# Expert stage: a fifth PSUM bank for the up products, one bank for both kinds of transpose, down products five units behind

## The reference, cut to what matters

```python
h = jax.nn.silu(jnp.einsum('ech,ehf->ecf', buf, w1))      # 8 experts, 128 -> 512
out_buf = jnp.einsum('ecf,efh->ech', h, w2)               # 512 -> 128
pair_out = out_buf[flat_e, slot] * keep[:, None]
combined = jnp.sum(pair_out.reshape(N, K, H) * k_probs[..., None], axis=1)
...
x = x + s * silu(combined + xn)
```

## Time and profile before

| | |
|---|---|
| median of 3 runs | 1129.29 us (1127.92 to 1129.47) |
| profiled execution, its own time | 1126.79 us |
| its span, first to last instruction | 1125.0 us |
| TensorE busy in the span | 993.5 us (88%) |
| VectorE, ScalarE, GpSimd busy | 832.7, 775.5, 644.6 us |
| mean granted TensorE clock, full is 1 | 0.968 |
| expert phase's blocks | 935 us to 1092 us from the span's start |

### The profile page before, as it was taken

How to read it: one execution, slowest core, us unless ns; L and a number is a source line. 1 busy time by engine, 2 the same in 40 slices (tenths; PEclk the granted TensorE clock), 3 DMA queues, 4 the chain that set the end, 5 groups by cost and what they waited for, 6 DMA issues and landing times. The chain is left out here.

```text
span 1125.0 us, 18399 instructions
## 1 busy us (share of the span) xinstructions
PE 993.5 (88%) x5064; PEld 426.3 (38%) x5064; DVE 832.7 (74%) x1591; ACT 775.5 (69%) x1524; POOL 644.6 (57%) x781
## 2 busy tenths in 40 slices
PE   4699999998999999869999999999999977888860
PEld 3123333333333332213344444444444354544430
DVE  4588888897888888748777767777777664565555
ACT  1067777776777777647788888888888666676651
POOL 6444545362636333336669787787878640655565
PEclk9999999999999999979999999999999998999995
DMA  2553836041314131369977886877887327112136
GB/s 58 97 89 102 186 98 131 21 81 42 59 28 71 43 48 46 105 184 272 228 206 200 236 231 182 237 208 198 227 226 205 87 89 246 54 57 78 28 99 241
DMA packets 102378, 149.78 MB, mean 133 GB/s; under 512 B 18216, under 2 KB 72088, under 8 KB 101838
## 3 DMA queue, kind: packets, MB, share of 16 engines
q1 hardware_dynamic: 95470, 139.65, 47.2%
q0 software_dynamic: 6272, 8.94, 2.8%
q10 hardware_dynamic: 544, 0.13, 0.2%
HBM read 109.44 MB, written 40.04 MB: 133 GB/s over the span
## 5 line engine op out<-in xcount | busy, mean ns | idle before, releaser
L811 ACT ACTIVATE a_probs<-a_score 128x512 f32<-128x512 f32 x512 | 291.9, 598 | 119.0 <-PE a_score L892 112.0
L987 DVE TENSOR_REDUCE a_mx<-a_mxps 128x2 f32<-128x1024 f32 x256 | 306.6, 1211 | 51.3 <-PE a_mxps L883 46.5
L1585 POOL TENSOR_TENSOR m_hidl<-m_hid,m_hidh 128x512 f16<-128x512 f32 x203 | 234.4, 1168 | 74.4 <-ACT m_hidh L1648 67.0
L1654 ACT ACTIVATE m_h<-m_h 128x512 f32<-128x512 f32 (+1 forms) x264 | 153.7, 583 | 48.7 <-PE m_h L1772 42.6
L1868 DVE TENSOR_TENSOR m_hid<-m_h,p_gates 128x512 f32<-128x512 f32 x196 | 134.0, 688 | 65.2 <-ACT m_h L1654 58.7
L904 PE MATMUL a_ops<-a_probs,a_vst 128*32 128x512 f32 x1024 | 138.1, 612 | 0.0
L1648 ACT ACTIVATE m_hidh<-m_hid 128x512 f16<-128x512 f32 x203 | 126.2, 622 | 11.0 <-DVE m_hid L1868 10.5
L1750 PE MATMUL m_y<-m_hidh,p_wdh 128*128 128x512 f16 (+1 forms) x264 | 100.3, 380 | 9.9 <-POOL m_hidl L1585 7.8
L2154 POOL DMA_INDIRECT t_picked<-e_yrow,p_rows x66 | 65.8, 998 | 75.2 <-DVE e_yrow L2289 55.6
L892 PE MATMUL a_score<-a_qstack,a_kstack 128*128 128x512 f16 x256 | 97.6, 387 | 6.7 <-ACT a_probs L811 3.5
L2302 DVE SCALAR_TENSOR_TENSOR e_hidl<-e_h,e_hidh 128x468 f16<-128x468 f32 (+1 forms) x96 | 57.5, 603 | 60.6 <-ACT e_hidh L2170 47.6
(11 more groups left out here) (308 smaller groups left out, 1933.1 us busy)
## 6 DMA issues: line engine op xcount, KB each, us to landing
p_gates<-t_cw SPq DMA_DIRECT2D x256, 256.0 KB
t_slots<-p_blank SPq DMA_DIRECT2D x8, 723.9 KB
t_qparts<-a_qparts SPq DMA_DIRECT2D x32, 128.0 KB
t_picked<-p_blank SPq DMA_DIRECT2D x8, 512.0 KB
p_raw<-up SPq DMA_DIRECT2D x8, 512.0 KB, 4.9
p_raw<-down SPq DMA_DIRECT2D x8, 512.0 KB, 5.1
p_rows<-t_slots SPq DMA_DIRECT2D x5, 723.9 KB
a_xin<-x SPq DMA_DIRECT2D x8, 256.0 KB, 5.0
```

The source lines that it names most:

```text
L811: act.activation(probs[:, kt % 2, g, :], score[:, g % 2, :], ACT.Exp, scale=SCALE / (QS * QS)).then_inc(exp_done, 1)
L987: dve.tensor_reduce(mx[ahead % 2][:, j // 2, g:g + 2], mxps[:, j % 2, :, :], AX.X, ALU.max).then_inc(mx_done, 1)
L1585: pool.tensor_tensor(hidl[0:r0, k % r, :], hid[0:r0, k % r, :], hidh[0:r0, k % r, :], ALU.subtract).then_inc(lo_done[0], 1)
L1654: act.activation(h, h, ACT.Silu, scale=1.0 / WS).then_inc(silu_done, 1)
```

## The change

`h` gets a fifth bank (`XBANKS` 5), which is taken from the transposes: both kinds now write one bank, `turned`. `down` runs 5 units behind `up` instead of 4. As the transposes share a bank, each kind waits until the other kind's last content has been read: `rows_turned(B)` for `row_done` of block B - 4, `result_turned(B)` for `xl_done` of block B + 3. In the orders, `result_out(B-2)` now comes at f = 0 instead of `result_out(B-1)` at f = 3; `result_turned(B-2)` and `result_rows(B-2)` move from f = 1 to f = 2; `split_weights` moves from f = 2 to f = 1. The final sum over pieces uses five banks as well.

```diff
-XLAG = 4
-XBANKS = 4
+XLAG = 5
+XBANKS = 5
...
-        xps, ops = ps("x", [P, 512]), ps("o", [P, 512])
+        turned = ps("x", [P, 512])
+        xps, ops = turned, turned
...
-                if f == 3 and B:
-                    result_out(B - 1)
+                if f == 0 and B >= 2:
+                    result_out(B - 2)
             high_part(FC * ALL - 1)
+            result_out(ALL - 2)
             result_out(ALL - 1)
...
+                if B >= 4:
+                    pe.wait_ge(row_done, B - 3)
                 for t in range(nt):
                     op = pe.transpose(xps[:, CR * t:CR * t + CR], rows_in[e % XBUFS][:, t0 + t, 0:D], ident[0:CR, 0:CR])
...
                 pe.wait_ge(yc_done, B + 1)
+                pe.wait_ge(xl_done, min(B + 4, ALL))
...
-                if f == 1 and B >= 2:
+                if f == 2 and B >= 2:
                     result_turned(B - 2)
-            result_turned(ALL - 2)
             for g in range(FC * ALL - XLAG, FC * ALL):
                 down(g)
+                if g == FC * ALL - XLAG + 2:
+                    result_turned(ALL - 2)
...
-                if f == 2 and B in SPLIT_IN:
+                if f == 1 and B in SPLIT_IN:
                     split_weights(dve, pre, JOBS + 1 + SPLIT_IN[B])
-                if f == 1 and B >= 2:
+                if f == 2 and B >= 2:
                     result_rows(B - 2)
```

## The result

The changed kernel takes 1153.07 us, the median of four executions, against 1129.11 us of the kernel before in the same session. One of the four took 1514.9 us at a mean granted clock of 0.659, and without it the median is 1150.55 us and the ratio to the kernel before 1.0203, 95% interval 1.0175 to 1.023. The two intervals don't overlap: the kernel before was some 4 us faster in the later session, so the size of the loss is known as 2.0 to 2.6% and no better. It is slower, as forecast; the forecast was 1166 us, with 1147 us for the case that no increment of TensorE is late any more.

The account below looks back on a forecast made before the run. TensorE was taken as the bound. Terms summed to +55.1 us with increments as late and +17.6 with none late; the middle, +36.4 on 1126.8, made 1163.2, and the median standing 2.5 higher gave 1166 us, range 1144 to 1187.

Parts of the forecast that it names:

- nothing late: End of the range where no TensorE increment is late any more: +17.6 us in sum, 1147 us.
- The deciding wait: At block start, TensorE's `rows_turned(B+1)` waits for DVE's `result_rows(B-3)` on the shared bank: 20 stops, 39.1 us.
- The split of the weights: `split_weights` at f = 1 delays DVE's low part in blocks 4, 7 and 10: +2.8 us, between 0 and 5.7.
- The late increments: TensorE's increments reach ACT late at eight places: +7.1 us if they stay as late, -17.2 if they vanish.
- The clock: TensorE's clock falls after long pauses: +5.6 us if increments stay late, -4.2 if none is late.
- my row: Profile row: 13 matmuls against 22 in the next 3.4 us stretch, so a clock fall costs 1.4 us.
- The other new wait: `result_turned` waiting for `x_low`: costed at nothing, with a thin cover of 0.6 us.
- The end: Time until block 20's rows are written: -2.9 us with nothing late, +0.5 with block 22's late place kept.
- A slow clock at every stop: Rival: stops of 1.6 to 2.2 us suffice to slow the clock, +59.7, 1189 us; chance 0.13.
- The covered stop: Rival: `result_rows` is done before TensorE arrives, so the ring's 9 us is had, 1120 us; chance 0.04.
- The third rival: Stops replace the pauses, increments never late: even at 1129 us if a stop costs under 1.1 us; chance 0.03.

Follow-up runs that it names:

- the later session: The unchanged changed kernel measured again beside other runs of the kernel before, giving its second trace: 1.026 (1.0245 to 1.0275), 1153.94 us.
- the variant with four banks: Changed kernel, its order and shared transpose bank kept, with XBANKS and XLAG 4 instead of 5: 1.0269 of the kernel before, 1153.65 us.
- the one with separate banks: Changed kernel's order and lag of five, but two separate transpose banks without the two new waits and four up-product banks: 0.9974, 1120.88 us.
- four variants with a pause at the start of nearly every block: Changed kernel with four banks, 1.0269; with split_weights behind result_rows, 1.021; with DVE's old order, 0.9927; kernel before with a wait in blocks 3 to 22, 1.0017.
- the variant with the rows first: Changed kernel with DVE's result_rows moved ahead of the low part of unit 4B+1: 0.9972 of the kernel before, 1121.37 us.
- the variant with three forced pauses: Kernel before with an added TensorE wait for the low part of unit 4B-2 at blocks 6, 12 and 18 only: 1.0006, 1125.49 us.

## Why the prediction was right, and where its size came from

The direction and the mechanism were right, the size was half as large again as measured: +36.4 us forecast, +23.8 between the profiled executions. The range held it, near its end for nothing late.

**The deciding wait: right, to a few hundredths.** The stops were forecast at 1.73, 2.20 and 1.93 us of lost pace, or 1.57, 2.04 and 1.77 as the trace counts idle time (0.16 less, the pipelined end). The trace has 1.57, 2.02 and 1.75, twenty of them, and that no other part of the change causes them is shown by the variant with four banks and by the one with separate banks. The pace lost is 39.6 us of idle time and 0.15 or 0.16 us for each restart (a matmul's record is 0.36 long while at full pace the next starts 0.20 after it), 42.8 us. The term was 39.1 for the plain stops and 2.8 for the split, 41.9.

**The split of the weights: a little under.** It lengthened three stops from 1.75 to 3.08, 4.0 us instead of 2.8. The second trace has 2.65, which makes 2.7 us, so the term is within what two traces differ by.

**The late increments: the term that made 1166 of 1147.** I had +7.1 if they stayed and -17.2 if they vanished, and took the middle for want of a row. They vanished. That is the term that was mis-sized: it went in at the middle, -5, and measured -17.2 (-19.5 with the restarts, below). The range held because it spanned both ends, not because the prediction knew which end would come. The row was there in part, as I had noted that lateness began at least 6 us after a pause, while the changed kernel runs some 5.4 us at a stretch; the bound was not turned into a weight. The runs show what was behind it: the increments were late only with all of POOL's indirect transfers and a TensorE that had no pause in each block. The changed kernel and four variants with a pause at the start of nearly every block, of 0.3 to 3.1 us, had no late place from block 3 on. Where TensorE's increments wait, and for what, is not shown by any of these runs.

**The clock: wrong.** I said that pauses up to 2.17 us leave the clock alone, and that none of the falls would be left if nothing was late: -4.2. The changed kernel has five falls where the kernel before has three after a pause: three after the stops that the split lengthens, but two after plain stops of 2.02 us, while most stops of the same length have none. In its second trace all five follow plain stops of 2.0. So the length of a single pause doesn't decide. Other traces say the same: a pause of 1.91 us in the variant with the rows first was followed by a fall, one of 2.77 us in the variant with three forced pauses was not. A fall cost 1.68 us, not 1.4. The Trainium skill, "TensorE: Matmul & The Clock Gate", Part 1 and its glossary, gives the penalty as throttled time times (1 - K/N), where K of N clock pulses are let through, 4 of 8 at the lower level: 1.7 us for 3.4. Here the changed kernel's trace agrees with the page, and my row, which compared matmul counts of neighbouring stretches, was too low. Four of the falls lie before unit 88, one more than before: +1.7 us.

**The other new wait.** Costed at nothing, and it was met once, in block 2, for 1.2 us. After that never.

**The end.** -2.9 forecast for nothing late, -1.4 measured to block 20's rows, and the rest of the span 0.9 longer. The fifth fall of the clock lies in this stretch, just behind the start of unit 88; at 1.68 us it is about the whole miss, so the term itself was right.

**The sum again, to unit 88.** 42.8 of stops, -17.2 of old pauses, +1.2, +1.7 of the clock make 28.5; the landmarks give 26.6. The 2 us between them are the restarts of the old pauses: the new stops were counted with 0.16 us for each restart, the old ones without. Between the landmarks there are twelve old pauses, the eleven of the 17.2 us and one of 0.39, so with their restarts 17.2 + 0.4 + 1.9 = 19.5 us went away, and the sum is 26.4 with the restart of the one other new wait. With -2.4 before the first up product, -1.4 and +0.9 it is the measured 23.8. The sum for nothing late had come to 17.6: of the missing 6 us, the clock is about as much by itself (I took 4.2 off, and it was 1.7 more by unit 88, with the fifth fall behind it); the smaller misses have both signs.

**The rivals.** A slow clock at every stop didn't happen: two of seventeen plain stops in the first trace, five of seventeen in the second. The covered stop is what the variant with the rows first makes; but the gain that I gave it, 9 us for the fifth bank, isn't there: it was 0.9972 with five banks and 0.9973 with four. The third rival, that it comes out even, had its condition met, as nothing was late any more, but at 2.1 us of lost pace a stop cost twice the 1.1 us that it allowed. The kernel before with a pause of 0.9 to 1.5 us in each block is close to that price, and it came out even, at 1.0017.

## What to carry to other kernels

When two buffers are put into one, write down for each new wait the last instruction that has to be through, which engine's order it stands in, and what the waiting engine still has to do by then: the cost per round can be read to a few hundredths of a microsecond from the trace of the kernel before. A late semaphore can be the real bound of a pipeline that looks limited by TensorE: look for products that ended long before their reader began, and ask what the other engines issue at that time. And an order written by hand should be redone after its banks change: the same banks cost 2.0 to 2.6% or gave 0.7%, by where DVE's rows stood.

## What the runs showed of the hardware

In the kernel before, TensorE's semaphore increments reached ACT up to 4.5 us late while POOL issued indirect transfers 1.3 us apart, three or four to a block, and TensorE ran without a pause. With half of the transfers or with plain transfers the longest wait for them was 0.4 us, and with pauses of 0.3 to 1.5 us once a block no Silu was over 1 us behind. After a forced pause it took nine units, 12.5 us, until lateness began again, and after a pause that late increments had caused mostly less, down to 6 us.

The granted clock fell to 1.2 GHz for 3.4 us after some pauses of 2.02 us and not after others of the same length. It fell after all three of 3.08 us and after none of the three of 2.65. Between the traces of other variants it is the same: it fell after one of 1.91 us and not after one of 2.77. In the variant with three forced pauses it fell twice at two shorter pauses close together, of 1.18 and 1.45 us and of 1.54 and 1.43 us. The length of a pause alone doesn't tell.
